# First attention of a four-layer decoder kernel: which engine copies the turned probabilities out of PSUM

## The reference, cut to what matters

```python
qkv = x @ W_attn + b_attn            # x: 4 x 512 x 128, after a layer norm
q, k, v = jnp.split(qkv, 3, axis=-1) # then split into 16 heads of 8
att = jnp.einsum('bqhd,bkhd->bhqk', q, k) * scale
att = att / temperature
bias = slopes[:, None, None] * rel[None, :, :]
bias = jnp.where(causal[None, :, :], bias, -jnp.inf)
w = jax.nn.softmax(att + bias[None, :, :, :], axis=-1)
y = jnp.einsum('bhqk,bkhd->bqhd', w, v).reshape(Bc, Tc, Cc)
return y @ W_proj + b_proj
```

## Time and profile before

| what | value |
|---|---|
| median of three executions | 2660.39 us (2655.98 to 2660.68) |
| the profiled execution | 2660.01 us |
| its span, first to last instruction | 2658.2 us |
| mean granted TensorE clock | 0.902 of full speed |
| TensorE busy, instructions | 2227.7 us (84%), 13502 |
| VectorE busy, instructions | 1791.3 us (67%), 3827 |
| ScalarE busy, instructions | 1241.8 us (47%), 2557 |
| GpSimd busy, instructions | 1196.4 us (45%), 1377 |

### The profile page before, as it was taken

How to read it: one execution, slowest core, us unless ns; L and a number is a source line. 1 busy time by engine, 2 the same in 40 slices (tenths; PEclk the granted TensorE clock), 3 DMA queues, 4 the chain that set the end, 5 groups by cost and what they waited for, 6 DMA issues and landing times. The chain is left out here.

```text
span 2658.2 us, 43969 instructions
## 1 busy us (share of the span) xinstructions
PE 2227.7 (84%) x13502; PEld 1582.2 (60%) x13502; DVE 1791.3 (67%) x3827; ACT 1241.8 (47%) x2557; POOL 1196.4 (45%) x1377
## 2 busy tenths in 40 slices
PE   6888759663999975749999999989999867699698
PEld 3666547453788853636656556655666445499555
DVE  4667658556688856666776676767677555477598
ACT  6777535222566642225445344534444432244365
POOL 5331028001699920127666565756575100022298
PEclk8999869775999998769999999999999977699799
DMA  1000024000666600013344343334333400000184
GB/s 45 2 2 2 7 57 100 7 6 19 140 153 153 150 4 18 1 63 80 80 84 92 77 98 75 96 65 96 77 84 79 87 6 0 32 1 1 25 176 101
DMA packets 63008, 162.17 MB, mean 61 GB/s; under 512 B 7563, under 2 KB 18571, under 8 KB 55000
## 3 DMA queue, kind: packets, MB, share of 16 engines
q1 hardware_dynamic: 62792, 159.50, 26.8%
HBM read 156.46 MB, written 3.01 MB: 60 GB/s over the span
## 5 line engine op out<-in xcount | busy, mean ns | idle before, releaser
L1984 PE MATMUL bank<-l2h_og,l2h_wo 128*128 128x512 f32 x512 | 264.2, 600 | 12.0 <-DVE LNT L2228 11.3
L2086 ACT ACTIVATE l2h_pr<-twin,l2h_nmx 128x512 f32<-128x512 f32 x256 | 176.0, 688 | 173.6 <-PE bank L1973 122.3
L2078 ACT ACTIVATE l2h_prT<-bank 128x512 f32<-128x512 f32 x256 | 151.7, 592 | 213.1 <-PE bank L1973 213.1
L1075 POOL TENSOR_TENSOR l1m_hid_lo<-l1m_hid,l1m_hid_hi 128x512 fp32r<-128x512 f32 x136 | 217.2, 1617 | 62.1 <-ACT l1m_hid_hi L1054 61.4
L2231 DVE TENSOR_REDUCE l2h_nmx<-twin 128x2 f32<-128x1024 f32 x128 | 156.2, 1220 | 104.5 <-PE twin L1963 103.8
L2204 DVE TENSOR_TENSOR l2h_vg<-bank,l2h_gv 128x512 f32<-128x512 f32 x256 | 175.4, 685 | 54.6 <-POOL l2h_vs L2299 32.0
L2299 POOL TENSOR_TENSOR l2h_vs<-l2h_vg 128x256 f32<-128x256 f32 x256 | 190.8, 745 | 27.9 <-DVE l2h_vg L2204 27.7
L2294 POOL TENSOR_TENSOR l2h_plain<-l2h_plain,l2h_rotated 128x512 f32<-128x512 f32 x64 | 82.0, 1281 | 213.9 <-DVE l2h_rotated L2197 213.9
L2216 DVE TENSOR_TENSOR l2h_og<-bank,l2h_gt 128x512 f32<-128x512 f32 x256 | 173.2, 680 | 5.3 <-PE bank L1984 2.7
L1973 PE MATMUL bank<-ident,l2h_pr 128*128 128x128 f32 x1024 | 163.4, 282 | 2.5 <-issue 2.5
L1973 PEld LDWEIGHTS bank<-ident,l2h_pr 128*128 128x128 f32 x1024 | 119.0, 143 | 71.4 <-issue 54.8
(11 more groups left out here) (636 smaller groups left out, 6199.1 us busy)
## 6 DMA issues: line engine op xcount, KB each, us to landing
l2h_gt<-l2m_gate_rows SPq DMA_DIRECT2D x128, 512.0 KB, 7.1
l1m_c<-l1m_weights SPq DMA_DIRECT2D x64, 512.0 KB, 6.3
l3m_c<-l3m_weights SPq DMA_DIRECT2D x32, 512.0 KB, 6.6
l0m_c<-l0m_weights SPq DMA_DIRECT2D x16, 512.0 KB, 6.8
l1m_w<-in_l1m_pairs SPq DMA_DIRECT2D x32, 192.0 KB, 6.2
l2h_fresh<-in_l2m_wqkv SPq DMA_DIRECT2D x8, 768.0 KB, 4.9
l2h_wo<-in_l2m_wo SPq DMA_DIRECT2D x8, 512.0 KB, 4.8
l0m_w<-in_l0m_pairs SPq DMA_DIRECT2D x8, 192.0 KB, 5.0
```

The costliest lines, as they stand in the source:

```text
L1075: nc.gpsimd.tensor_tensor(hid_lo[:, at, :], hid[:, (n + PRE) % 4, :], hid_hi[:, at, :], ALU.subtract)\
L1984: nc.tensor.matmul(ybank[:, :], wo[s][:, e, :], og[:, e % 4, :], start=(e == 0), stop=(e == E - 1))\
L2078: nc.scalar.activation(prT[:, j // 2 % 2, h, :, j % 2 * P:(j % 2 + 1) * P], tbank[:, :].rearrange("p (c q) -> p c q", c=TPB), ACT.Copy).th ...
L2086: nc.scalar.activation(pr[:, h, :], sbank[:, h, :], ACT.Exp, bias=nmx[:, k % 2, h:h + 1], accum_out=rs[:, g % 2, t, h:h + 1]).then_inc(exp ...
```

## The change

Copy 1 of each quad moves from VectorE to ScalarE. On ScalarE it stands behind exponential 0 of the step and ahead of copy 2; the order becomes copy 0, exponential 0, copies 1 and 2, exponentials 1, 2, 3. On VectorE the order becomes masks 0, 1, 2, 3, copy 3. `copy` on ScalarE picks the bank by the head's parity. The counts that TensorE waits for follow: three copies a quad are counted on `copied_a`, one on `copied_v`.

```diff
@@ VectorE
                     if k < QUADS:
                         mask(k, 0)
-                    if 1 <= k <= QUADS:
-                        copy(k - 1, 1)
                     if k < QUADS:
                         for r in range(1, R):
                             mask(k, r)
@@ ScalarE
-                    nc.scalar.activation(prT[:, j % RING, r, 0:W], tbank[0][:, 0:W], ACT.Copy).then_inc(copied_a, 1)
+                    nc.scalar.activation(prT[:, j % RING, r, 0:W], tbank[r % 2][:, 0:W], ACT.Copy).then_inc(copied_a, 1)
...
                     if k < QUADS:
                         exponent(k, 0)
                     if k >= 1:
+                        copy(k - 1, 1)
                         copy(k - 1, 2)
@@ TensorE, turn
-                    before = 2 * j + r // 2
-                    if before:
-                        pe.wait_ge(copied_v if r % 2 else copied_a, before)
+                    if r == 1:
+                        if j:
+                            pe.wait_ge(copied_v, j)
+                    elif 3 * j + r:
+                        pe.wait_ge(copied_a, (3 * j, 0, 3 * j + 1, 3 * j + 2)[r])
@@ TensorE, weigh
-                    pe.wait_ge(copied_a, 2 * j + 2)
-                    pe.wait_ge(copied_v, 2 * j + 2)
+                    pe.wait_ge(copied_a, 3 * j + 3)
+                    pe.wait_ge(copied_v, j + 1)
```

## The result

The changed kernel takes 2692.53 us (median of four executions, 2689.66 to 2694.64), the kernel before 2659.22 us (median of four). The ratio is 1.0126, with a 95% interval of 1.0109 to 1.0144. It is 33 us slower; 2691 was forecast. The profiled execution took 2689.66 us over a span of 2687.9 us, 29.7 us longer than the span before.

A forecast was written before the change was run, and what follows sets the result against it. TensorE was taken as nearest to full, waiting mostly for ScalarE's copies (23.6 us). Head 3's late turn, 29 us, plus 2 us of clock gave 31 us on 2660: 2691 us, 1.2% slower, range 2680 to 2707.

The forecast's parts named there:

- The place in the queue: On ScalarE copy 1 stands behind exponential 0, so TensorE turns head 3 0.41 to 0.58 us later per step: 29 us.
- The steps that finish a tile: VectorE's relief does not help where a reciprocal delays it; head 3's turn comes 0.64 us later at W = 512.
- Nobody absorbs it: TensorE's work after head 3's turn follows in program order, so the whole 29.0 us lies on the path.
- ScalarE's load: ScalarE still fits its fullest steps, about 4.2 us at W = 256, with less to spare; nothing added.
- The copy's own price: At 512 columns 0.60 us on ScalarE, 0.69 on VectorE, quoted reason ScalarE is closer to PSUM; worth nothing by itself.
- The clock: TensorE idles more, so two more steps at half clock: +2 us, bounds a 4 us gain to a 10 us loss.
- The rival's 2703 to 2712 us: Half of the 24 steps with a projection lose 0.9 us each at lower clock, 11 us more; chance 0.12.
- The rival's condition: VectorE's relief decides, 6 to 10 us faster, only if copy 1 precedes exponential 0 or that never waits; chance 0.03.

The follow-up runs named there:

- E1: Changed kernel, but copy 1 stands ahead of exponential 0 on ScalarE: 2648.49 us, ratio to the kernel before 0.9959.
- E3: Changed kernel, but copy 1 stands behind copy 2 on ScalarE, same load: 2742.22 us, ratio to the kernel before 1.0319.
- E4: Kernel before, with mask 1 ahead of copy 1 on VectorE and no work moved between engines: 2677.50 us, ratio 1.0072.
- E2: Kernel before, plus one copy-wide ScalarE instruction per step behind exponential 3, written to an unread buffer: 2659.20 us, ratio 1.0006.
- E6: Changed kernel, with TensorE doing `weigh` between the turns of heads 1 and 2: 2648.56 us, ratio to the kernel before 0.9954.
- E5: Kernel before, with TensorE doing `weigh` between the turns of heads 1 and 2: 2637.76 us, ratio 0.9915.
- E7: E1 with TensorE doing `weigh` between the turns of heads 1 and 2: 2639.52 us, ratio to the kernel before 0.9920.
- E8: Changed kernel, but copies 0 and 1 on ScalarE ahead of exponential 0, copies 2 and 3 on VectorE behind masks 2 and 3: 2652.13 us, ratio 0.9969.

## Why the prediction was right

**The place in the queue, 29 us.** Right, in mechanism and size. The parts of the sum can be read off step by step (start of the scores of one step to that of the next, before and after): 4.85 to 5.41 us at W = 512, 4.75 to 5.24 at W = 384, 3.80 to 4.23 at W = 256: 0.56, 0.49 and 0.43 against 0.58, 0.47 and 0.41. At W = 128 it is 3.33 to 3.73, 0.40 against 0.42. In the 50 steps at full clock in both traces the mean delay is 0.49 us, against 29.5/63 = 0.47. E1 shows the cause by undoing it alone, E3 by adding to it, E4 by making it on the other engine.

**The steps that finish a tile.** 0.64 us was forecast for W = 512; 5.26 to 5.85 us was measured, 0.59.

**Nobody absorbs it.** Right: 31.3 us in the stage.

**ScalarE's load.** Counted as nothing. For this kernel that was right within the noise of the medians: E2's load shows as 2.8 us in its trace, in steps with a piece of projection, and in the changed kernel the steps at W = 384 with a piece grew by 0.48 us, those without by 0.49. E6 shows where it matters: once the wait is covered, the fullest steps feel load and place together.

**The copy's own price.** Worth nothing by itself, as forecast. The reason that the prediction quotes for ScalarE's shorter copy is not what the rows show. On average a copy takes 0.27 us on ScalarE and 0.29 on VectorE at 128 columns, and 0.60 and 0.69 at 512. The difference grows from 0.01 to 0.09 us, so nearly all of it is time for each column, 0.84 ns against 1.04, and not a fixed cost of each copy.

**The clock, 2 us.** The size came out in the profiled execution; the cause stays open, and some of the agreement is luck. The 61 steps between the third and the last grew by 31.1 us; at 0.49 us a step that is 29.9, and 1.2 us are left. One step alone, at 196 us, grew by 2.13 in place of some 0.5, since the clock came back later; where the first steps and the falls that were there before lay in half clock, some steps grew by less. But E2, in which no wait was removed, has 7 us less of half clock than the kernel before, so a difference of 10 us between two traces may not come from the change. The rule of the Trainium skill that was weighed here (page "TensorE: Matmul & The Clock Gate", section "HAM oscillation — how this bites in real kernels") agrees best with E3, where the idle time grew further. Its own case is waits for DMA that are longer than TensorE's waits here (for a copy in E3 1.4 us at most), and E4 does not fit it: its waits are longer than those before, and it is at half clock for 20 us. The rival's 2703 to 2712 us hold 3 to 12 us beyond its terms (29 and 11 on 2660.4) that no row gives. Its price for a step was low: the step at 196 us took 5.28 us at half clock, its like at full clock 3.65, so 1.6 us and not 0.9.

**Two terms under the uncertainty.** The medians differ by 33.3 us, the profiled executions by 29.7. The other executions after are up to 5 us longer than the profiled one at a slightly lower mean clock (0.899 against 0.901), which fits more half clock in them, but they have no trace.

The weak spot of the prediction was the other side: it read the waits that VectorE's queue causes in steps that finish a tile off the profile's names. They are worth 6.2 us in E1's trace, not the 3.7 us that stood under VectorE. The rival's condition, copy 1 ahead of exponential 0, was stated, its price was set at 6 to 10 us, and E1 measured 10.5, of which 2.9 us in its trace are clock.

## What to carry to other kernels

When work moves to an engine with spare time, ask first what it stands behind in that engine's queue and who waits for it; the busy share of the two engines said nothing here (29 us of work in idle time cost at most some 3 us, one place in the queue, between the changed kernel and E1, 44 us). Put what another engine waits for ahead of what nobody waits for yet, then look for independent work to cover what is left: on TensorE that gave the best kernel here, 2637.8 us, 0.8% below the one before. A wait may stand under the name of the last of several releasers, so a step that has it and one that has not should be compared by their length.

## What the runs showed of the hardware

TensorE's clock stood at half for different times in this stage, though the steps do the same work: 14 us in E5, 17 in E1, E2, E6 and E7, 20 in E4 and E8, 24 before, 34 with the change and 72 in E3, each in one trace. The two longest times go with the longest waits for ScalarE's copies (52 and 83 us). Below that there is no such order: in E2 TensorE waits longer in all than in the kernel before, with 7 us less of half clock, and E4 has longer waits and 3 us less. No long pause is needed for a fall: in the 7 us before each of the three falls after the first three sequences the longest pause of TensorE was 0.6 us before the change and 1.0 to 1.2 us after it.

A step with a projection at W = 256 took 5.28 us at half clock and 3.65 at full clock, both with the change. The price of a wait on TensorE can therefore be more than its length, as in E3: 50 us for 40, or for 35 by its own steps at full clock.
